# Three transformer blocks and a spectral block on one core: operands in one arena, V's bias folded away, LN in three parts, and every dense step for one image by a table of times

## The chip, the cores and the metric

The kernel runs on one core of a Trainium2 chip, in one launch. The time is the device time of an execution in microseconds; the figure shown is the median of several executions. The profile is of one further execution, taken by the hardware profiler. Its engines are TensorE (PE, with its weight loads as PEld), VectorE (DVE), ScalarE (ACT), GpSimd (POOL) and SyncE (SP), which here issues all DMAs.

## The reference

The input is x, 4 images of 16 x 16 tokens with 192 channels, in float32. Four blocks follow one another, each with its own weights.

```
for layer in (0, 1, 2):                 # head size 16, 48, 16; window 14, 16, 14
    y = layernorm(x) * g1 + b1
    q, k, v = split(windows(y) @ w_qkv + b_qkv)     # 12 heads
    a = (q * scale) @ k.T + rel_h(q)[..., None] + rel_w(q)[..., None, :]
    x = x + (softmax(a) @ v) @ w_proj + b_proj
    x = x + gelu((layernorm(x) * g2 + b2) @ w1 + b1) @ w2 + b2   # 192 -> 768 -> 192
# layer 3, spectral: rfft2 over the image, two complex 8-block matrices with biases,
# relu between them, soft shrink (0.01) after, inverse rfft2, added to x
```

With window 14 an image of 16 x 16 falls into one full window (196 tokens) and three that are mostly padding. Padded tokens are keys too: their k and v are the biases alone.

## The kernel before

Work goes in six phases: layers 0, 1 and 2, each for the first two images and then for the other two (`Phase`). Phases 0, 1, 4 and 5 have heads of 16 and windows of 14 (`L14`, `pads`), phases 2 and 3 have heads of 48 and one window of 16 (`L16`). Tokens of two images make 512 columns, four tiles of 128.

The steps of a phase are: `ln` (statistics, 1/sqrt by an integer guess and three Newton steps, normalisation, all on VectorE), `turn` (TensorE transposes, ScalarE writes XT with scale and bias), `q` and `k` (chunks of 96 columns of weights), `qs` and `ks` (each of q and k split in a high and a low part), `rel` (small matmuls with the relative positions), `aug` (SP copies the split parts and the relative terms of one head into its operand slot, QA and KA, beside rows of constants), `max` (scores once, VectorE takes the maxima of the rows), `maxT` (the maxima are transposed, and SP copies them as one more row, NR to QA), `scores` (scores again, less their maximum, and exp on ScalarE into PT), `pv`, `copy_o`, `inverse` and `divide` (output of a group of heads and its division by the sums), `norm` (the same for the last group), `proj`, the second `ln` and `turn`, `up`, `gelu`, `down`. The spectral block has `fwd`, `s1`, `s2`, `inv`, `out`.

Each engine takes its instructions in order, and all walk the same list of steps: `ordered()` (L298). A phase's frame is its scores, head by head; `attention_slots` hangs max (three heads ahead, or two), maxT, pv and aug on it; `beside(p)` spreads the tail of the phase before and the head of the next over the first three quarters, by costs written at each step. Where the layer changes (phases 2 and 4), `constants` and `prelude` come behind all of it: every row of constants, every slot's operands and the first maxima of the new layer are issued after the old layer's last scores. SP waits for those scores by name (L639 to L641, L682).

Slots: 6 for heads of 16, 4 for heads of 48, in two pairs of tensors (QA14 and KA14, QA16 and KA16) that share one place. Three banks of PSUM (`DENSE`) go round among the dense steps; two hold maxima, two scores, one the outputs.

The lines that matter below: L600 to L602 and L686 to L701 (weights, on the same SP queue as operands and rows), L766 (GpSimd permutes XT to XP for V and K of the 14-windows), L837 (K), L872 (exp), L890 and L896 (up, gelu), L899 (an Exp of two elements, which brings Exp's table back), L953 to L974 (LN), L980 (VectorE waits for the columns of layers 1 and 2), L1001 (V with its bias), L1005 to L1017 (q's split), L1043 (maxima), L1122 (every matmul).

Of the kernel before, what the change touches and what calls it, by code (L numbers as in the profile page):

```python
# [16 lines left out]
HB = 2  # L17
# [27 lines left out]
class Layer:  # L45


    def __init__(self, index, head_dim, window, eps, gelu):
# [150 lines left out]
def head_steps(p):  # L199

    L = PHASES[p].L
    out = [(("ln", 0, 0), 5.0), (("turn", 0, 0), 3.0)]
    if L.pads:
        out += [(("q", 0, 0), 1.0), (("k", 0, 0), 1.0), (("qs", 0, 0), 0), (("ks", 0, 0), 0), (("q", 1, 0), 1.5)]
        out += [(("rel", i, 0), 1.5) for i in range(3)]
    else:
        out += [(step, d) for step, d in unit_steps(0)]
    return out


def unit_steps(i):

    a, b = 2 * i, 2 * i + 1
    return [(("q", a, 0), 1.5), (("qs", a, 0), 0), (("q", b, 0), 1.5), (("k", a, 0), 1.5), (("ks", a, 0), 0),
            (("rel", i, 0), 2.0), (("qs", b, 0), 0), (("k", b, 0), 1.5), (("ks", b, 0), 0)]


def tail_steps(p):

    out = [(("proj", 0, 0), 1.5), (("proj", 1, 0), 1.5), (("ln", 1, 0), 5.0), (("turn", 1, 0), 3.0)]  # L220
    out += [(("up", m, 0), 1.5) for m in range(FM)]
    out += [(("gelu", 0, 0), 0), (("gelu", 1, 0), 4.0)]
    return out + [(("down", k, 0), 2.0) for k in range(2)]


def spectral_steps(s):
    out = [(("fwd", u, 0), 1.2) for u in range(4)] + [(("s1", u, 0), 1.2) for u in range(4)]
    return out + [(("s2", u, 0), 1.5) for u in range(4)] + [(("inv", t, 0), 1.5) for t in range(4)] + [(("out", 0, 0), 0)]


def beside(p):

    out = []
    if p:
        out += [((p - 1, *step), d) for step, d in tail_steps(p - 1)]
    if p % 2 == 0:
        out.append(((p, "weights", 0, 0), 0))
    if p == 5:
        out += [((4, *step), d) for step, d in spectral_steps(0)]
    if p + 1 < 6:  # L240
        out += [((p + 1, *step), d) for step, d in head_steps(p + 1)]
    return out


def attention_slots(p):

    L = PHASES[p].L
    slots = {(h, k): [(p, "scores", h, k)] for h in range(HEADS) for k in range(L.units)}
    joined = p + 1 < 6 and PHASES[p + 1].L is L
    for h in range(HEADS):  # L250
        g, first = h // L.per_group, h % L.per_group == 0
        if first and g:
            for k in range(L.units):
                slots[h, k].append((p, "pv", g - 1, k))
            slots[h, L.units - 1].append((p, "copy_o", g - 1, 0))
            slots[h + 1, 0].append((p, "inverse", g - 1, 0))
            slots[h + 1, L.units - 1].append((p, "divide", g - 1, 0))
        m = h + L.ahead
        where = (p, m) if m < HEADS else (p + 1, m - HEADS) if joined else None
        if where:  # L260
            for k in range(L.units):
                slots[h, k].append((where[0], "max", where[1], k))
            late = (h + 1, 0) if h + 1 < HEADS else (h, L.units - 1)
            slots[late].append((where[0], "maxT", where[1], 0))
        a = h + L.ring
        if a < HEADS:
            slots[h, L.units - 1].append((p, "aug", a, 0))
        elif joined and a - HEADS < L.ring:
            slots[h, L.units - 1].append((p + 1, "aug", a - HEADS, 0))
    if not L.pads:  # L270
        for i in range(1, 3):
            work = [(p, *step) for step, _ in unit_steps(i)]
            at = range(0, 4) if i == 1 else range(4, 12)
            for j, step in enumerate(work):
                k = at[j * len(at) // len(work)]
                slots[k // 2, k % 2].append(step)
    return [slots[h, k] for h in range(HEADS) for k in range(L.units)]


def prelude(p):  # L280

    L = PHASES[p].L
    out = [(p, "aug", h, 0) for h in range(L.ring)]
    for h in range(L.ahead):
        out += [(p, "max", h, k) for k in range(L.units)]
        if h:
            out.append((p, "maxT", h - 1, 0))
    return out + [(p, "maxT", L.ahead - 1, 0)]


FILL = [0.75] * 6


def second_chunk(p):
    return [(p, "k", 1, 0), (p, "qs", 1, 0), (p, "ks", 1, 0)] if PHASES[p].L.pads else []


def ordered():  # L298

    out = [(0, *step) for step, _ in head_steps(0)]  # L300
    out += prelude(0)
    for p in range(6):
        L = PHASES[p].L
        if p and PHASES[p - 1].L is not L:
            out += [(p, "constants", 0, 0), *prelude(p)]
        out += second_chunk(p)
        out += [(p, "v", t, 0) for t in range(L.vtiles)]
        slots, extra = attention_slots(p), beside(p)
# [33 lines left out]
def _build(nc, ctx, io, out):  # L342
# [180 lines left out]
    def split_rooms(L, c):  # L523

        if L.pads:
            return QHL14[:, :, :], KHL14[:, :, :]
# [892 lines left out]
```

## Time and profile before

| | |
|---|---|
| median of 3 runs | 798.07 us (797.04 to 798.78) |
| the profiled execution's own time | 794.48 us |
| its span, first to last instruction | 792.7 us |
| granted TensorE clock, mean over the span | 0.825 of full speed |
| HBM read and written | 10.09 MB and 0.79 MB |
| DMA bytes in all, mostly copies within the core | 51.73 MB |

The profile gives each engine's busy time and its share of the span. A wait is the idle time of an engine ahead of an instruction, put down to what came last. The granted clock is a share of TensorE's full 2.4 GHz; its other level is half of it. Every float32 matmul shows as two instructions, each with its weight load.

### The profile page before, as it was taken

Reading aid. Unit: us, or ns where it says so; the run is one execution under the profiler, and the core shown is the slowest. Engines: PE = TensorE matmul, PEld = TensorE weight load, DVE = VectorE, ACT = ScalarE, POOL = GpSimd, SP = SyncE. Lnnn points to the kernel's source line nnn. Section 1 sums busy time; section 2 is a strip of 40 time slices with the busy share of each in tenths; the row PEclk is TensorE's granted clock in tenths of the full one; section 3 lists DMA queues with packets and bytes.
Section 4 is the critical chain, followed back from the end, with each engine's and each line's share of the span. In section 5 each row is a group of like instructions: output and inputs, shape, how many; then the busy total and the mean of one; then the engine's idle time right before and its main releaser. Section 6 shows DMA issues by size and latency. Waiting matters only on the chain.

```text
span 792.7 us, 13858 instructions
## 1 busy us (share of the span) xinstructions
PE 601.9 (76%) x5444; PEld 434.8 (55%) x5444; DVE 314.9 (40%) x846; ACT 224.7 (28%) x420; POOL 125.1 (16%) x154
## 2 busy tenths in 40 slices
PE   7737487797906988878989887387949667997677
PEld 4525365666605645645755655265726454785366
DVE  4325546526212521515242363535344652352203
ACT  2113231263400235213124433003523226222231
POOL 2120202000400231132032230010011210010001
PEclk8666756698856999979989997678986779997799
DMA  5582122130033122344022130612251302100000
GB/s 159 135 197 58 39 59 57 24 72 21 14 86 114 31 80 74 104 121 132 15 75 72 47 104 2 170 27 49 47 145 41 77 19 58 39 2 20 1 0 21
DMA packets 31913, 51.73 MB, mean 65 GB/s; under 512 B 8383, under 2 KB 12719, under 8 KB 31754
## 3 DMA queue, kind: packets, MB, share of 16 engines
q1 hardware_dynamic: 31850, 50.85, 24.8%
q8 instruction: 44, 0.72, 0.4%
q14 instruction: 19, 0.16, 0.1%
HBM read 10.09 MB, written 0.79 MB: 14 GB/s over the span
## 4 chain that ended last, share of the span: by engine, by line
PE 59%; DVE 16%; SPq 8%; DMA 7%; issue 5%; ACT 5%; DVEq 0%; POOL 0%; ACTq 0%
PE PS L1122 56%; DVE NM L1043 3%; DMA QA<-NR 3%; DMA COL<-in_col 2%; DVE STAT L954 2%; PE PS L1140 1%; DMA QA<-KC 1%; SPq L615 1%; PE PS L1214 1%; DVE XN L973 1%; DVE QHL L1016 1%; ACT HT L896 1%; SPq L654 1%; SPq L648 1%; DVE RSTD L965 1%
## 5 line engine op out<-in xcount | busy, mean ns | idle before, releaser
L872 ACT ACTIVATE PT<-PS 98x392 f32<-98x392 f32 (+2 forms) x192 | 96.2, 513 | 319.1 <-PE PS L1122 318.6
L1043 DVE TENSOR_REDUCE NM<-PS 98x2 fp32r<-98x392 f32 (+2 forms) x192 | 108.1, 572 | 146.4 <-PE PS L1122 145.0
L1122 PE MATMUL PS<-QA,KA 128*98 128x196 f32 (+2 forms) x528 | 124.8, 348 | 28.3 <-DMA QA<-NR 20.3
L1122 PE MATMUL PS<-KA,QA 127*98 127x196 f32 (+3 forms) x432 | 105.5, 344 | 48.5 <-issue 33.9
L1122 PEld LDWEIGHTS PS<-QA,KA 128*98 128x98 f32 (+2 forms) x528 | 89.9, 212 | 58.5 <-issue 24.7
L1122 PEld LDWEIGHTS PS<-KA,QA 127*98 127x98 f32 (+3 forms) x432 | 72.8, 217 | 69.8 <-issue 50.2
L1122 PE MATMUL PS<-XT,W 96*128 96x512 f32 x144 | 69.9, 620 | 1.3 <-ACT XT L817 1.3
L1122 PE MATMUL PS<-XT,WQKV 96*96 96x512 f32 x128 | 64.7, 635 | 1.3 <-ACT XT L817 1.3
L1214 PE MATMUL PS<-IDN,NM 120*6 120x120 f32 (+1 forms) x72 | 22.9, 318 | 54.4 <-DVE NM L1043 54.4
L1122 PE MATMUL PS<-PT,V 128*32 128x196 f32 (+2 forms) x672 | 60.6, 407 | 0.9 <-ACT PT L872 0.9
L1122 PE MATMUL PS<-W,HT 128*128 128x192 f32 x288 | 52.6, 343 | 10.9 <-ACT HT L896 10.9
L1122 PEld LDWEIGHTS PS<-W,HT 128*128 128x128 f32 x288 | 50.2, 202 | 13.6 <-ACT HT L896 12.6
L771 POOL TENSOR_TENSOR OT<-OS,OT 128x512 f32<-128x512 f32 x18 | 23.0, 1276 | 205.7 <-DVE OT L1061 205.6
L1051 DVE CAST NR<-PS 5x120 fp32r<-5x120 f32 (+1 forms) x72 | 19.0, 264 | 63.0 <-PE PS L1214 56.1
L1122 PEld LDWEIGHTS PS<-XT,W 96*128 96x128 f32 x144 | 27.1, 199 | 28.5 <-issue 26.6
L1122 PE MATMUL PS<-Q,RB 32*32 32x32 f32 (+1 forms) x2304 | 37.7, 225 | 5.0 <-issue 4.1
L1214 PEld LDWEIGHTS PS<-IDN,NM 120*6 120x6 f32 (+1 forms) x72 | 5.9, 83 | 61.5 <-DVE NM L1043 61.5
L1122 PEld LDWEIGHTS PS<-Q,RB 32*32 32x32 f32 (+1 forms) x2304 | 34.8, 126 | 8.6 <-issue 7.5
L1122 PEld LDWEIGHTS PS<-PT,V 128*32 128x32 f32 (+2 forms) x672 | 28.4, 137 | 18.5 <-issue 6.7
L1122 PE MATMUL PS<-WP,OT 128*128 128x192 f32 x192 | 36.0, 351 | 3.0 <-DVE OT L1075 3.0
L1122 PEld LDWEIGHTS PS<-WP,OT 128*128 128x128 f32 x192 | 35.1, 210 | 4.2 <-issue 4.2
L890 ACT ACTIVATE HT<-PS,COL 128x512 f32<-128x512 f32 x36 | 24.7, 687 | 43.0 <-PE PS L1122 43.0
(91 smaller groups left out, 663.2 us busy)
## 6 DMA issues: line engine op xcount, KB each, us to landing
QA<-QHL SPq DMA_DIRECT2D x72, 96.0 KB, 2.4
KA<-KHL SPq DMA_DIRECT2D x48, 141.0 KB, 2.6
QA<-REL SPq DMA_DIRECT2D x48, 128.0 KB, 2.4
QA<-QHL SPq DMA_DIRECT2D x24, 192.0 KB, 2.7
KA<-KHL SPq DMA_DIRECT2D x24, 192.0 KB, 2.7
W<-in_w SPq DMA_DIRECT2D x6, 576.0 KB, 6.5
QA<-REL SPq DMA_DIRECT2D x48, 64.0 KB, 2.2
KA<-KC SPq DMA_DIRECT2D x12, 235.0 KB
```

The costliest lines, as they stand in the source:

```text
L615: sp.dma_start(raw(KA16[row:end, tile, s, :]).rearrange("r (b t) -> r b t", b=HB), KC16[L.rel_row:L.rel_row + size, :].unsqueeze(1).broadc ...
L648: sp.dma_start(raw(QA14[0:3 * hd, 0, s, :]), raw(qhl[mine, :, :])).then_inc(aug_in[s].sem, 16)
L654: sp.dma_start(raw(KA14[0:3 * hd, 0, s, :]), raw(khl[mine, :, :])).then_inc(aug_in[s].sem, 16)
L771: nc.gpsimd.tensor_tensor(OT[:, i, :], OS[:, :], OT[:, i, :], ALU.mult).then_inc(o_done.sem, 1)
L872: nc.scalar.activation(dst, src, ACT.Exp).then_inc(probs_done.sem, 1)
L890: nc.scalar.activation(HT[:, i, :], PS[:, bank[0], :], ACT.Identity, bias=COL[n][:, b1:b1 + 1])\
L896: nc.scalar.activation(part, part, L.gelu).then_inc(gelu_done.sem, 1)
L954: ins = nc.vector.bn_stats(STAT[:, t, :], X[:, t0 + t, :])
L1043: nc.vector.tensor_reduce(dst, src, AX.X, ALU.max, negate=True).then_inc(max_done.sem, 1)
L1051: nc.vector.tensor_copy(NR[0:cols, h % 2, 0:L.max_rows], PS[0:cols, bank[0], 0:L.max_rows])\
L1122: return nc.tensor.matmul(dst, lhsT, rhs, start=start, stop=stop, skip_group_check=loose)
L1214: nc.tensor.transpose(PS[0:cols, bank[0], 0:rows], NM[n][0:rows, h % 2, 0:cols].bitcast(F32), IDN[0:rows, 0:rows]).then_inc(maxT_psum.sem, 1)
```

## The change

The diff replaces the order of the steps, the place of the operands and the split of several steps.

1. **Order.** `head_steps`, `tail_steps`, `beside`, `attention_slots`, `prelude` and `second_chunk` go. A table `TIMES` holds for each phase and step the times at which its instances stand, in heads, counted from 12p; `scores` stand at h + k / units. `ordered()` sorts by them.
2. **One image.** `ln`, `turn`, `up`, the first two chunks of `q` and the first of `k` are done for one image (256 columns) at a time, as is `s1`. The gelus of the two images are separate, each with its return to Exp. ScalarE evacuates up of the first image, VectorE that of the second. XT1 is one tensor in place of two. The spectral block has its own room (LATE) for each half.
3. **Arena.** Operand slots of both layers lie in one tensor, 5 for heads of 48 and 6 for heads of 16, so that a new layer's slot waits only for the old heads that lie under it. Constants are laid slot by slot (a pair of slots in one DMA for heads of 16). Q and K parts of a head of 16 go in one DMA.
4. **Fold.** V's bias is no longer added to V. It is multiplied into the projection (`fold`) and added to the row of its bias; the padded values become zeros and a one.
5. **Split normalisation.** `ln` is VectorE's statistics, `rs` GpSimd's 1/sqrt, `xn` ScalarE's normalisation. `norm` is two steps.
6. K of the 14-windows is made from unpermuted columns and permuted as ScalarE writes it; V of these layers is written by ScalarE. PT16 has four rooms in place of two. X's second half and the columns of layers 1 and 2 are loaded at phase 0's `weights` step, ahead of the weights. The memsets of PT14 go.

```diff
-        self.ring = 6 if self.pads else 4
+        self.ring = 6 if self.pads else 5
+        self.turn = 2 if self.pads else 3
+        self.slot_room = self.tiles * (HT_ + self.keys)
-        self.aug_dmas = 3 if self.pads else 6
+        self.aug_dmas = 2 if self.pads else 6
...
+def place_of(p, h):
+    L = PHASES[p].L
+    return (HEADS * (p % 2) + h + L.turn) % L.ring
+
+def slot_start(L, s):
+    return L16_ROOM - (L.ring - s) * L.slot_room
...
+TIMES = [
+    {"ln": (-7.429, -7.238, 13.611, 14.190,),
+     "rs": (-7.810, -7.048, 13.889, 14.286,),
+     "xn": (-7.619, -6.667, 14.143, 14.513,),
...
+     "k": (-6.476, -4.762, 0.444,),
...
+     "v": (-0.571, 0.167, 1.042, 1.083, 1.208,),
+     "weights": (2.889,),
...
+    {"ln": (-8.917, -6.200, 13.700, 14.417,),
...
+     "aug": (-4.167, -3.067, -2.111, -1.111, -0.111, 0.200, 1.190, 2.095, 3.111, 4.143, 5.133, 6.250,),
...
+     "constants": (-2.800, -1.933, -1.600, -0.111, 0.125,),
+     "aug": (-2.733, -1.733, -1.222, 0.312, 0.929, 1.900, 2.812, 3.750, 4.938, 5.577, 6.889, 7.700,),
...
+def ordered():
     out = []
+    for p, table in enumerate(TIMES):
         L = PHASES[p].L
+        scores = tuple(h + k / L.units for h in range(HEADS) for k in range(L.units))
+        for step, times in [("scores", scores), *table.items()]:
+            out += [(HEADS * p + t, (p, step, *part)) for t, part in zip(times, parts(L, step, len(times)))]
+    return [step for _, step in sorted(out, key=lambda timed: timed[0])]
...
             elif step == "constants":
-                sp.wait_ge(*scores_psum.at(p - 1, HEADS * PHASES[p - 1].L.units - 1))
-                lay_constants(ph)
+                s = place_of(p, h)
...
+                over = last_over(p, s) if p else None
...
+                if over is not None:
+                    sp.wait_ge(*scores_psum.at(p - 1, PHASES[p - 1].L.units * (over + 1) - 1))
+                if not L.pads or h % 2 == 0:
+                    lay_constants(L, s)
...
+            elif step == "rs":
+                pool.wait_ge(*mean_var[i].at(p, u))
+                two_tiles = slice(2 * u, 2 * u + 2)
+                var, rstd, sq = VAR[:, two_tiles], RSTD[:, two_tiles], SQ[:, two_tiles]
+                link(nc.gpsimd.tensor_scalar(var, MV[:, two_tiles, 1], L.eps, None, ALU.add))
+                link(nc.gpsimd.tensor_scalar(rstd.bitcast(I32), var.bitcast(I32), -0.5, float(0x5F3759DF),
+                                             ALU.mult, ALU.add))
+                for _ in range(3):
+                    link(nc.gpsimd.tensor_tensor(sq, rstd, rstd, ALU.mult))
+                    link(nc.gpsimd.tensor_tensor(sq, sq, var, ALU.mult))
+                    link(nc.gpsimd.tensor_scalar(sq, sq, -0.5, 1.5, ALU.mult, ALU.add))
+                    link(nc.gpsimd.tensor_tensor(rstd, rstd, sq, ALU.mult))
+                link(nc.gpsimd.tensor_tensor(sq, rstd, MV[:, two_tiles, 0], ALU.mult))
+                nc.gpsimd.tensor_scalar(sq, sq, -1.0, None, ALU.mult).then_inc(rstd_done[i].sem, 1)
...
+            if step == "xn":
+                act.wait_ge(*rstd_done[s].at(p, u))
...
+                for t in range(2 * u, 2 * u + 2):
+                    nc.scalar.activation(XN[:, t, :], X[:, ph.tile0 + t, :], ACT.Identity, scale=RSTD[:, t:t + 1],
+                                         bias=SQ[:, t:t + 1]).then_inc(xn_done[s].sem, 1)
...
             elif step == "gelu":
-                if i == 0:
-                    act.wait_ge(*up_done.at(p, FM - 1))
+                act.wait_ge(*up_done[i].at(p, FM - 1))
...
-                if i == 1:
-                    nc.scalar.activation(LOADED[:, :], COL[0][:, 0:2], ACT.Exp)
+                nc.scalar.activation(LOADED[:, 1 + 2 * p + i, :], COL[0][:, 0:2], ACT.Exp)
...
+            elif step == "up" and u == 1:
+                dve.wait_ge(*up_psum.at(p, FM + i))
+                nc.vector.tensor_scalar(HT[:, i, TOK:], PS[:, bank[0], 0:TOK], COL[n][:, b1:b1 + 1], None, ALU.add)\
+                    .then_inc(up_done[1].sem, 1)
+            elif step == "fold":
+                dve.wait_ge(*fold_psum.at(p, 0))
+                nc.vector.tensor_tensor(WP[rows, 0, :], WP[rows, 0, :], PS[rows, bank[0], 0:C], ALU.add)\
+                    .then_inc(fold_done.sem, 1)
```

## Rows read from the trace of the kernel before

**Rows 1.** The page's first part: busy us, share of the span, instructions
```profile
PE 601.9 (76%) x5444; PEld 434.8 (55%) x5444; DVE 314.9 (40%) x846; ACT 224.7 (28%) x420; POOL 125.1 (16%) x154
```
**Rows 2.** Windows by stage (one without matmuls left out): us, busy us per engine, clock, DMA share, GB/s
```profile
0.00:64.50 64.50, 35.19 (x488) 23.54 (x488) 26.97 (x96) 10.16 (x23) 12.24 (x34) 0.69 0.60 151
64.50:218.60 154.10, 123.87 (x1300) 92.97 (x1300) 71.45 (x180) 56.31 (x117) 23.41 (x25) 0.75 0.20 45
...
242.60:498.70 256.10, 222.63 (x2028) 153.56 (x2028) 98.48 (x263) 76.34 (x126) 58.93 (x61) 0.91 0.25 73
498.70:525.20 26.50, 11.63 (x34) 6.54 (x35) 15.09 (x26) 0.98 (x2) 3.66 (x3) 0.63 0.55 137
525.20:726.60 201.40, 158.52 (x1394) 121.78 (x1394) 86.28 (x232) 66.79 (x133) 22.27 (x26) 0.85 0.20 49
726.60:792.70 66.10, 50.08 (x200) 36.41 (x200) 14.17 (x45) 14.09 (x19) 4.54 (x5) 0.87 0.02 6
```
**Rows 3.** Waits of TensorE: engine line, for whom, us in total, times, longest
```profile
PE PS L1214 <- DVE NM L1043: 54.4, 29, 18.3
PE PS L1122 <- issue: 46.0, 10, 24.0
PE PS L1122 <- DMA QA<-NR: 20.3, 8, 7.7
PE PS L1122 <- DVE V L1001: 13.4, 4, 6.1
PE PS L1122 <- ACT HT L896: 10.9, 5, 3.6
```
**Rows 4.** Timeline, start: start us, us, engine, line, what, idle before, releaser
```profile
37.22 3.64 PE L1122 MATMUL PS<-XP,WQKV 96*96 96x512 f32 x4
...
40.65 3.85 PE L1122 MATMUL PS<-WQKV,XP 96*98 96x192 f32 x20
...
44.78 0.88 ACT L872 ACTIVATE PT<-PS 98x392 f32<-98x392 f32 x2 [2.83 <-PE PS L1122]
```
**Rows 5.** The chain of waits, then the timeline, behind phase 0's weights
```profile
45.21 13.10 DMA COL<-in_col
...
64.53 0.36 PE L1214 MATMUL PS<-IDN,NM 120*6 120x120 f32 x1 [18.30 <-DVE NM L1043]
```
**Rows 6.** Timeline at the boundary to phase 2: an issue of SP, TensorE's wait
```profile
236.67 0.61 SPq L650 DMA_DIRECT2D QA<-QHL  x1
...
242.60 2.05 PE L1122 MATMUL PS<-KA,QA 128*128 128x256 f32 x8 [24.04 <-issue]
```
**Rows 7.** Timeline, second chunk's split in phase 1
```profile
95.12 0.36 PE L1214 MATMUL PS<-IDN,NM 120*6 120x120 f32 x1 [9.80 <-DVE NM L1043]
```
**Rows 8.** Timeline, first and last of the six waits for an LN
```profile
153.18 0.36 PE L1214 MATMUL PS<-IDN,NM 120*6 120x120 f32 x1 [5.32 <-DVE NM L1043]
...
738.58 2.08 PE L1140 MATMUL PS<-IDN,XN 128*96 128x128 f32 x8 [5.12 <-DVE XN L973]
```
**Rows 9.** Timeline of ScalarE at a gelu
```profile
172.38 1.28 ACT L896 ACT_TABLE_LOAD   x1
...
173.68 2.86 ACT L896 ACTIVATE HT<-HT 128x1536 f32<-128x1536 f32 x2
```
**Rows 10.** Timeline: a load of up, and 128 Q,RB matmuls twice
```profile
751.31 0.19 PEld L1122 LDWEIGHTS PS<-XT,W 96*128 96x128 f32 x1 [0.24 <-issue]
...
101.38 2.12 PE L1122 MATMUL PS<-Q,RB 32*32 32x32 f32 x128
...
271.47 2.06 PE L1122 MATMUL PS<-Q,RB 96*32 96x32 f32 x128
```
**Rows 11.** Groups by form: count, busy us, mean ns, idle before
```profile
L973 DVE TENSOR_SCALAR XN<-X,MV,RSTD 128x192 f32<-128x192 f32 x48 | 15.0, 376 | 0.4
```
**Rows 12.** GpSimd: a memset in the timeline, and a group by form
```profile
59.28 0.12 POOL L734 MEMSET BV<- 120x12 f32 x1
...
L786 POOL TENSOR_SCALAR W1N<-WS 96x192 f32<-96x192 f32 x1 | 0.7, 692 | 15.3 <-DMA SB<-in_sb 15.3
```

More of the change, by code:

```diff
@@ L218, in tail_steps @@
[L218 to L228, printed above, removed]
@@ L231, in beside @@
-def beside(p):
-    out = []
[L234 to L277, printed above, removed]
@@ L280, in prelude @@
[L280 to L302, printed above, removed]
-        L = PHASES[p].L
[L304 to L308, printed above, removed]
-        whole, at, placed = sum(d for _, d in extra) / FILL[p], 0.0, []
-        for step, d in extra:
-            placed.append((at / whole * len(slots), step))
-            at += d
-        for j, slot in enumerate(slots):
-            out += slot
-            while placed and placed[0][0] < j + 1:
-                out.append(placed.pop(0)[1])
-        out += [step for _, step in placed]
-        out += [(p, "pv", L.groups - 1, k) for k in range(L.pv_steps)] + [(p, "norm", 0, 0)]
-    out += [(5, *step) for step, _ in tail_steps(5)]
-    return out + [(5, *step) for step, _ in spectral_steps(1)]
@@ L323, with last_over @@
-BANKS = {"turn": 2, "q": 1, "k": 1, "rel": 1, "maxT": 1, "proj": 1, "up": 1, "down": 1, "fwd": 1, "s1": 1, "s2": 1,
+    return (HEADS * (p % 2) + h + L.turn) % L.ring
+def slot_start(L, s):
+    return L16_ROOM - (L.ring - s) * L.slot_room
+L16_ROOM = LAYERS[1].ring * LAYERS[1].slot_room
+def last_over(p, s):
+    L, before = PHASES[p].L, PHASES[p - 1].L
+    first, end = slot_start(L, s), slot_start(L, s) + L.slot_room
+    over = [h for h in range(HEADS - before.ring, HEADS)
+            if slot_start(before, place_of(p - 1, h)) < end
+            and slot_start(before, place_of(p - 1, h)) + before.slot_room > first]
+    return over[-1] if over else None
@@ new lines, in parts @@
+def parts(L, step, n):
+    if step in ("max", "scores", "pv"):
+        per_head = L.pv_steps if step == "pv" else L.units
+        return [divmod(j, per_head) for j in range(n)]
+    if step in ("ln", "rs", "xn", "turn"):
+        return [divmod(j, HB) for j in range(n)]
+    if step == "up":
+        return [(m, b) for b in range(HB) for m in range(FM)]
+    if step == "q":
+        return [(c, b) for b in range(HB) for c in range(2)] + [(c, HB) for c in range(2, L.chunks)]
+    if step == "k":
+        return [(0, b) for b in range(HB)] + [(c, HB) for c in range(1, L.chunks)]
+    return [(j, 0) for j in range(n)]
@@ L351, in _build @@
     XN = sb(ctx, "XN", [128, 4, C])
-    XT1 = [sb(ctx, f"XT1_{half}", [CK, 2, HT_]) for half in range(2)]
+    XT1 = sb(ctx, "XT1", [CK, 2, HT_])
     XT2 = sb(ctx, "XT2", [CK, 2, HT_])
@@ L541, in values @@
     def values(L, t, h):
-        rows = EDGES if L.pads and t == 2 * HB else 128
+        rows = 128 if not L.pads else HALF_IN if t < 2 * HB else EDGES
         return V[L.index][0:rows, t, h * L.vcol:h * L.vcol + L.slot]
@@ L966, in _ @@
[L966 to L984 removed]
+                ins.then_inc(mean_var[s].sem, 1)
@@ L1384, in _pack @@
         place[0, L.sum_row, 0] = bp
+        vb = np.zeros((L.per_group, L.slot, L.groups, L.sum_row + 1), np.float32)
+        bv = bqkv[2 * L.dim:].reshape(L.groups, L.per_group, L.hd).transpose(1, 2, 0)
+        for row, first, end in L.spans:
+            vb[:, row:row + end - first, :, L.sum_row] = bv[:, first:end]
         rb = np.zeros((pairs, L.hd, 2, 2, L.rel_room, 2), np.float32)
```

688 lines of the change are left out of this document (437 added, 251 removed).

## The prediction

> **What bounds the kernel now.** I read the page's first part, then the stages by windows, then TensorE's waits, then the timeline at each long wait. Over the 792.7 us span TensorE is busy 601.9 us, no other engine as much as 315 [rows 1]. So 190.8 us are TensorE's idle time. The windows cut the span where the work changes: start, phases 0 and 1, phases 2 and 3 (head size 48), the boundary to phase 4, phases 4 and 5, and the tail [rows 2]; between the second and the third lie 24.0 us without a matmul [rows 6]. The reader is to see two things in them: how much of each TensorE stands, and that the granted clock goes with how closely TensorE is fed: 0.69 and 0.75 in the first two stages, 0.91 in phases 2 and 3, where it is busy 87% of the time. Busy time times granted clock, summed over the six rows, is 24.3 + 92.9 + 202.6 + 7.3 + 134.7 + 43.6 = 505 us: what the same matmuls would take at 2.4 GHz. So 97 us of the busy time are the lower clock's. The two prizes are thus 191 us idle and 97 us of slow clock; beneath them lie some 505 us of work that the change hardly touches.
>
> The waits say who leaves TensorE idle [rows 3]: mostly VectorE's maxima (54.4 us in 29 waits), because VectorE takes its instructions in order and something else stands ahead of them; then "issue" (46.0 in 10), which is above all the two boundaries; then the row of maxima that comes by DMA (20.3), VectorE's copies of V (13.4) and the gelu (10.9).
>
> **The change part by part**, against the profiled execution (794.48 us, of which 792.7 span). Table entries are in heads: phase p counts from 12p, and one head takes about 6 us in phases 0, 1, 4, 5 and 10 us in 2 and 3 (201.4 and 154.1 us for about 24 heads each, 256.1 for 24).
>
> *Start.* The first exp is at 44.8; ahead of it stand the maxima of three heads, K's second chunk (3.64 us of matmul) and the V tiles (3.85 us) [rows 4]. By phase 0's table, K chunk 1 (0.444) and four of five V tiles (0.167 and later) come behind the first scores (0.0): -6.7 us. Six constant DMAs in place of twelve and a K that no longer waits for the permuted copy give some 2 more. I take **-9**; bounds 0 (the maxima alone set it) and -14 (twice what the two parts give).
>
> *Weights of phase 0.* TensorE idles 18.3 us up to 64.5, since VectorE waits 13.1 us for the column biases, queued behind weights [rows 5], and then does phase 1's LN before the maxima. Now X's second half and the columns are issued first (2.889), and VectorE's statistics wait (3.083) for X alone. But the weights still go by the one SP queue, and the next rows of maxima (maxT of head 5 at 3.167) queue behind them: the same megabytes held the queue for 13 us. I take **-10**, bounds -4 (13 of them return as waits for the row) and -16.
>
> *Boundaries.* 24.0 us at 218.6 [rows 6], and 14.9 idle in the 26.5 us behind 498.7 [rows 2]: all constants of the new layer, then all operands, wait for the old layer's last scores. In the arena, slots are freed one by one: phase 2's first head lies over L14 slots 2 to 4, free after head 8, the second over 4 and 5, free after head 9, the third over none; constants start at -2.8 and operands at -2.73. What remains is SP: three constant and six operand DMAs for each L16 head, at 0.61 us of issue and 0.03 between them [rows 6], are 5.8 us a head beside about 3 that an L14 head needs, in 6 us. So SP falls some 3 us behind with each of three heads: 9 us late on the 24, which leaves -15. At the second, whose new heads need less of SP, I take 10 of the 14.9: **-25**; bounds -10 (SP also waits in order for scores) and -36 (nearly all of both).
>
> *Second chunk's split, V, and XP.* 9.8 us at 85.3 [rows 7] are VectorE waiting for head 5's operand DMA before it may overwrite the split rooms, and then the split; the V copies cost 13.4 [rows 3], and about 6 us of "issue" are a wait for the permuted copy. V's copies go to ScalarE, K needs no permuted input. The room still waits for head 5 (issued at 0.2, split at 0.56 to 0.61, that is 2 us later with a landing of 2.5), so half stays: 29 us in all, **-14**; bounds -6 and -24.
>
> *LN.* A whole LN holds VectorE for about 5.3 us; six waits, of which the first and the last are shown, come to 30.4 [rows 8], and I add 4.5 for phases 2 and 3, where they are shorter. Now VectorE does only the statistics, for one image at a time (4 of the 24 instructions that held it, so about 0.9 us), GpSimd the 16 small operations, ScalarE the four normalisations. **-24** of 34.9; bounds -10 and -38.
>
> *Gelu.* Each image gets its own gelu and its own way back to Exp, so there are 12 more table loads at 1.28 us [rows 9], 15.4 us of ScalarE, which is idle 72% of the time. Waits for the gelu cost 10.9 us of TensorE now [rows 3]. The first gelu comes earlier, the second load costs again: **+6**, bounds 0 and +15 (nothing hidden). Here a page speaks against the change. The row shows the load from 172.38 and the gelu from 173.68, 1.30 us. The Trainium skill (ScalarE: Activation LUTs, What ACT_TABLE_LOAD costs) adds about 1.38 us of drain to each switch, 2.66 us in all. By that the twelve would be 32 us and my +6 about +12; the trace has no such gap, so the row is taken.
>
> *More and smaller matmuls.* Up goes from 12 to 24 matmuls a phase, q and the first k likewise, s1 from 16 to 32: with the fold some 270 instructions over 5444. At 2.4 GHz a 512-column pass has a pitch of 0.43 us (load 0.19, then 0.24 idle) [rows 10], so 256 columns take 0.215 and still cover the load. Taken as **0**; it would be +8 (0.03 each) were loads in the open. The six folds are in the last term.
>
> *Tail.* From 726.6 to the end 66.1 us, 50.1 busy. Phase 4's spectral part (16 fwd, 16 s1, 32 s2 and 32 inv instructions a half, at about a weight load's 0.2 us [rows 10] some 20 us of TensorE) moves from beside phase 5's heads (11.4 to 21.7 in phase 5's table) into the tail, whose holes come to 66.1 - 50.1 = 16 us [rows 2], 5.1 of them the LN [rows 8]. 20 us leave phase 5 and about 10 come back beyond the holes: **-10**, bounds 0 and -20.
>
> *What ScalarE takes over.* 48 normalisations (15.0 us on VectorE at 376 ns), 20 V copies, split turns, K in three pieces, less up's second image [rows 11]: some 25 us by an estimate from that 376 ns beside the table loads, on an engine that works in order between exps. The normalisation waits for GpSimd's chain. The nearest GpSimd rows are 0.12 us (memset 120x12) and 0.69 (96x192, one operand) [rows 12]; nearest in size is the first, so 16 x 0.15 to 0.2 = 2.4 to 3.2 us, against 0.35 to 0.45 head, 2 to 2.7 us, that the tables leave between the two steps. About 0.3 us late, 24 times, with the folds and the copies: **+11**, bounds 0 and +35. Beside it: the Trainium skill (GPSIMD Engine Reference, Performance versus the Vector engine) advises against GpSimd for elementwise work, at 1.96 times VectorE's time on large tiles; no row of before shows it at two columns.
>
> *Clock.* If every stage is fed as phases 2 and 3 are now, it gets their 0.91: 505 / 0.91 = 555 in place of 602, -47; less some 7, because the Q,RB matmuls take 2.1 us for 128 at either clock [rows 10]: **-40**. Bounds -10 (the waits move rather than go) and -65.
>
> Sum: -9 -10 -25 -14 -24 +6 +0 -10 +11 -40 = -115, or 679.5 us for a profiled execution. The median of the runs shown, 798.07, is 3.6 above the profiled 794.48, so I predict **683 us**.
>
> **The rivals.** *A: the waits go and the clock stays.* The same sum without the clock term gives 719.5, 723 as a median. For it: phases 4 and 5 have 21% idle and 0.85, so the clock isn't bound to a single long wait. Against: the clock is highest where the idle share is lowest. *B: TensorE becomes the whole limit.* 505 us of work, 15 for Q,RB and the like, and idle time of 35 at the start, 15 at boundaries, 20 in the tail and 5 in each of six phases give 620, 624 as a median. For it: no other engine passes 40%. Against: the chains exp, PV, maxima and SP's order stay. *C: ScalarE waits in order for GpSimd, and the kernel gets slower.* Place: step "xn", 24 times, each ahead of an exp that TensorE needs. If a GpSimd operation costs 0.69 us even at two columns, the chain is 11.0 us against 2.5 allowed: 8.5 late, of which some 2 are covered by the two score banks. 24 x 6.5 = 156, less the 7 already counted: 683 + 149 = 832. It passes "before" from a chain of about 9.3 us, 0.58 us an operation. For it: ScalarE and TensorE have at most two banks between them. Against: the memsets at 0.12. *D: the written order itself misfits* (SP at the boundaries, rows of maxima behind weights): half of the idle time returns elsewhere; 115 / 2 gives 741.
>
> **How the numbers follow.** 0.45 for my forecast (its own range 655 to 705), 0.20 for B, 0.17 for A, 0.11 for D, 0.07 for C. The range 632 to 742 leaves out most of C and the outer ends of B and D. Faster: everything but C, 0.93, less 0.01 for a chance landing within 0.2% (1.6 us, about what can be told from no change): faster 0.92, same 0.01, slower 0.07.
>
> **What would show it.** Right: no TensorE wait over 12 us at the two boundaries; VectorE's maxima end under 25 us of waits in place of 54; the first exp before 38 us; some 5700 matmul instructions; granted clock about 0.9 over the span; TensorE's busy time near 560. Wrong: a clock below 0.86 (A); xn instructions whose idle time before them is GpSimd's and longer than 2 us each (C); waits for the row of maxima above 35 us in all, or SP issuing without a break across the boundaries while TensorE stands (D). The sum fails if the tail grows by more than phase 5 loses.

## The result, and the profile after

The changed kernel takes 760.3 us (median of 4 runs, 758.13 to 764.34) against 797.59 of the kernel before beside it, a ratio of 0.9536 [0.9495, 0.9578]. The forecast was 683 with a range of 632 to 742: the direction was right, the size was a third. The profiled execution took 760.11 us. Now and then an execution is over 1.5% slower than the fastest of its kernel, mostly at a lower granted clock: times and ratios below (a ratio with its 95% interval) are of the others, and only the profiles of the wide relative terms (clock 0.822) and of the loads from ScalarE's queue (0.612) are of such executions.

The page's first part, columns as in [rows 1]:

```profile
span 758.3 us, 14860 instructions
PE 615.0 (81%) x5716; PEld 484.3 (64%) x5716; DVE 273.3 (36%) x671; ACT 279.5 (37%) x580; POOL 199.8 (26%) x540
```

TensorE's idle time fell from 190.8 us to 143.3, by 47.5. Its busy time rose by 13.1, though the forecast had it fall by 40. The granted clock is 0.835 over the span, against 0.825. The windows of the kernel after, columns as in [rows 2], cut at the first exp, inside phases 0 and 1, at the first boundary, at the first and last exp of phases 2 and 3, at the first and last exp of phases 4 and 5:

```profile
0.00:42.90 42.90, 30.04 (x467) 23.73 (x467) 10.77 (x36) 11.69 (x31) 13.74 (x54) 0.66 0.44 101
42.90:147.50 104.60, 70.64 (x801) 53.68 (x801) 44.70 (x108) 33.77 (x89) 21.94 (x54) 0.66 0.39 88
147.50:227.30 79.80, 68.08 (x545) 54.30 (x544) 26.19 (x70) 36.18 (x73) 23.35 (x75) 0.85 0.16 37
227.30:256.50 29.20, 23.75 (x255) 15.09 (x254) 8.77 (x20) 4.90 (x10) 5.03 (x5) 0.82 0.38 109
256.50:491.60 235.10, 205.10 (x1917) 157.70 (x1917) 84.95 (x199) 92.05 (x166) 80.33 (x187) 0.91 0.31 86
491.60:494.60 3.00, 1.40 (x10) 0.84 (x10) 1.53 (x4) 0.34 (x3) 0.00 (x0) 1.00 0.63 139
494.60:682.00 187.40, 153.16 (x1349) 122.95 (x1351) 74.48 (x185) 79.25 (x171) 42.09 (x123) 0.83 0.25 57
682.00:758.30 76.30, 62.86 (x388) 55.98 (x378) 21.89 (x51) 21.31 (x40) 13.34 (x42) 0.95 0.04 11
```

The kernel before had the same events at 44.8 (first exp), 260.1, 496.6, 528.5, 721.6 and 792.7. So the start is 1.9 us shorter, phases 0 and 1 with the first boundary 1.7 (213.6 against 215.3), phases 2 and 3 1.4, the second boundary 28.9 (3.0 against 31.9), phases 4 and 5 5.7, and the tail 5.2 longer. In sum 34.4, most of it at the second boundary, where the idle time fell from 15.1 us to 1.6 and some 15 us of TensorE's work now stand in other stages.

TensorE's waits after, columns as in [rows 3]:

```profile
PE PS L1320 <- ACT XN L983: 30.3, 12, 6.4
PE PS L1303 <- DMA ARENA<-NR: 26.8, 10, 12.8
PE PS L1395 <- DVE NM L1212: 21.5, 12, 6.2
PE PS L1303 <- issue: 21.0, 19, 5.3
PE PS L1303 <- DVE NM L1212: 11.3, 13, 2.6
```

The maxima's 54.4 us are 21.5, under the 25 of the forecast, and "issue" is 21.0 in place of 46.0, no wait of it over 5.35. The first exp (42.9, to be under 38), the clock and the busy time missed their signs. The first line is new: the transposes of the "turn" step wait for the normalisation. On ScalarE that is a wait for GpSimd, in the kernel after's groups (count, busy us, mean ns, idle before):

```profile
L983 ACT ACTIVATE XN<-X,SQ,RSTD 128x192 f32<-128x192 f32 x48 | 23.6, 538 | 68.2 <-POOL SQ L936 68.1
```

One of the 24 chains, in the timeline of the kernel after (start, length, engine; "..." stands for 13 more of GpSimd's operations of 0.19 or 0.20 us; work of other engines in between, and lines between the last three, are left out):

```profile
521.97 0.25 DVE L1147 BATCH_NORM_AGGREGATE MV<-STAT 128x2 f32<-128x6 f32 x2
522.31 0.22 POOL L927 TENSOR_SCALAR VAR<-MV 128x2 f32<-128x2 f32 x1 [17.81 <-DVE MV L1147]
522.61 0.19 POOL L928 TENSOR_SCALAR RSTD<-VAR 128x2 int32<-128x2 int32 x1
...
526.49 0.22 POOL L936 TENSOR_SCALAR SQ<-SQ 128x2 f32<-128x2 f32 x1
526.75 0.98 ACT L983 ACTIVATE XN<-X,SQ,RSTD 128x192 f32<-128x192 f32 x2 [4.72 <-POOL SQ L936]
527.87 1.06 PE L1320 MATMUL PS<-IDN,XN 128*96 128x128 f32 x4 [6.43 <-ACT XN L983]
530.40 6.33 PE L1303 MATMUL PS<-XT,W 96*128 96x256 f32 x16
537.38 1.97 PE L1303 MATMUL PS<-XT,W 96*128 96x256 f32 x8
```

Sixteen operations of two columns follow one another every 0.276 us (0.20 at work, 0.08 between), from 522.31 to 526.71: 4.4 us, and the other 23 chains take as long. ScalarE and TensorE take their steps in order, and both stand meanwhile. Of the 24 chains ScalarE waited for 17, TensorE for 12. The reader is to look at the last two lines too. The first 16 matmuls of up behind the wait take 0.396 us each, the next 8 of the same form 0.246. The windows around that place say why (same columns as above):

```profile
517.00:521.40 4.40, 4.40 (x30) 4.19 (x28) 1.05 (x3) 0.26 (x1) 0.00 (x0) 1.00 0.00 0
521.40:527.90 6.50, 0.07 (x2) 0.06 (x2) 2.10 (x11) 1.61 (x4) 3.20 (x17) 0.83 0.25 58
527.90:532.00 4.10, 4.10 (x16) 3.76 (x17) 1.52 (x3) 1.37 (x3) 3.14 (x12) 0.50 0.00 0
532.00:536.00 4.00, 4.00 (x11) 3.13 (x11) 0.00 (x0) 1.95 (x5) 2.00 (x6) 0.51 0.00 0
536.00:540.00 4.00, 4.00 (x25) 3.47 (x24) 0.45 (x2) 3.08 (x8) 0.00 (x0) 1.00 0.01 1
```

Full clock, a wait of 6.4 us, then 1.2 GHz for 8 us in which TensorE never stops, then 2.4 again. So the wait is paid for twice, and dense work stands behind it: up here, q/k elsewhere. They are the groups that carry the extra busy time, up at 79.1 us after (69.9 before) and q/k at 100.1 (86.6 before).

### The profile page after: what moved, and what is told of

Its sections match the earlier page's. It is cut to its first block, busy times and chain, and to the rows that moved or that the text cites. A ratio compares the mean times of both kernels' runs of the same rounds, so it can differ in the third digit from the quotient of the medians.

```text
span 758.3 us, 14860 instructions
## 1 busy us (share of the span) xinstructions
PE 615.0 (81%) x5716; PEld 484.3 (64%) x5716; DVE 273.3 (36%) x671; ACT 279.5 (37%) x580; POOL 199.8 (26%) x540
## 4 chain that ended last, share of the span: by engine, by line
PE 60%; DMA 9%; issue 8%; SPq 8%; DVE 6%; POOL 5%; ACT 3%; DVEq 0%; ACTq 0%; POOLq 0%
PE PS L1303 56%; DMA ARENA<-NR 4%; DMA ARENA<-REL 4%; PE PS L1320 2%; ACT XN L983 1%; DVE QKHL L1185 1%; PE PS L1395 1%; DVE NM L1212 1%; SPq L790 1%; DMA ARENA<-KC 1%; SPq L810 1%; DVE QKHL L1180 1%; POOL SQ L932 1%; SPq L812 1%; POOL RSTD L934 1%
## 5 line engine op out<-in xcount | busy, mean ns | idle before, releaser
L1303 PE MATMUL PS<-ARENA 128*128 128x256 f32 (+4 forms) x960 | 193.3, 339 | 52.3 <-DMA ARENA<-NR 26.8
L1303 PEld LDWEIGHTS PS<-ARENA 128*128 128x128 f32 (+4 forms) x960 | 149.0, 215 | 88.5 <-issue 33.2
L1303 PE MATMUL PS<-XT,WQKV 96*96 96x256 f32 (+1 forms) x232 | 100.1, 577 | 9.1 <-issue 7.8
L1303 PE MATMUL PS<-XT,W 96*128 96x256 f32 x288 | 79.1, 423 | 5.5 <-ACT XT L993 4.6
L1303 PEld LDWEIGHTS PS<-XT,W 96*128 96x128 f32 x288 | 59.1, 214 | 18.8 <-ACT XT L993 6.1
L1303 PEld LDWEIGHTS PS<-XT,WQKV 96*96 96x96 f32 x232 | 45.7, 212 | 38.4 <-issue 28.4
L1303 PE MATMUL PS<-PT,V 98*32 98x196 f32 (+2 forms) x672 | 57.1, 381 | 1.8 <-ACT PT L1051 1.8
L983 ACT ACTIVATE XN<-X,SQ,RSTD 128x192 f32<-128x192 f32 x48 | 23.6, 538 | 68.2 <-POOL SQ L936 68.1
L1320 PE MATMUL PS<-IDN,XN 128*96 128x128 f32 x96 | 20.6, 355 | 31.1 <-ACT XN L983 30.3
L1303 PE MATMUL PS<-Q,RB 32*32 32x32 f32 (+1 forms) x2304 | 38.5, 225 | 7.7 <-issue 6.4
L1395 PE MATMUL PS<-IDN,NM 120*6 120x120 f32 (+1 forms) x72 | 22.2, 310 | 22.9 <-DVE NM L1212 21.5
L1303 PEld LDWEIGHTS PS<-PT,V 98*32 98x32 f32 (+2 forms) x672 | 26.0, 127 | 19.7 <-issue 8.7
```

Source lines behind the costliest of these rows:

```text
L983: nc.scalar.activation(XN[:, t, :], X[:, ph.tile0 + t, :], ACT.Identity, scale=RSTD[:, t:t + 1], bias=SQ[:, t:t + 1]).then_inc(xn_done[s]. ...
L1303: return nc.tensor.matmul(dst, lhsT, rhs, start=start, stop=stop, skip_group_check=loose)
L1320: last = nc.tensor.transpose(PS[0:CK, bank[0], k * TOK + t * 128:k * TOK + (t + 1) * 128], XN[:, 2 * u + t, k * CK:(k + 1) * CK], IDN[:, :])
L1395: nc.tensor.transpose(PS[0:cols, bank[0], 0:rows], NM[n][0:rows, h % 2, 0:cols].bitcast(F32), IDN[0:rows, 0:rows]).then_inc(maxT_psum.sem, 1)
```

## The experiments

The theory after the comparison: GpSimd's chain makes the normalisation late, 24 times, and the lower clock behind each wait doubles the loss. The rival: such waits only move, and the clock is held down by something else (the small matmuls, the halved dense steps). All kernels are edits of the kernel after unless said otherwise; a ratio is to the kernel before beside it.

**Chain of 4 operations.** The three Newton steps are left out, so 1/sqrt is only the first guess.

```diff
-                for _ in range(3):
+                for _ in range(0):
                     link(nc.gpsimd.tensor_tensor(sq, rstd, rstd, ALU.mult))
```

> The kernel after, with the three Newton steps of 1/sqrt left out (so the normalisation keeps only the first guess): GpSimd's chain is 4 operations in place of 16, about 1.1 us in place of 4.4, 24 times. Theory 1 (the chain is what makes ScalarE's normalisation late, and TensorE stands and then runs at the lower clock): TensorE's waits for XN fall from 30.3 us to under 8, ScalarE's for GpSimd from 68 to under 15, the granted clock rises to 0.86 or more, the time falls by 35 us or more, to 725 or less. Theory 2 (TensorE's waits only move to the next late thing, and the clock has another cause): the XN waits go likewise, but others grow, the clock stays at 0.83 to 0.845 and the time stays at 745 or more.

720.4 us, 0.9054 [0.9022, 0.9086]: 40 us less for twelve operations a chain (38 by the ratios, each to the kernel before beside it).

```profile
span 717.3 us, 14572 instructions
PE 597.7 (83%) x5716; PEld 471.4 (66%) x5716; DVE 270.6 (38%) x671; ACT 278.7 (39%) x580; POOL 143.7 (20%) x252
```

The waits for XN are 8.0 us in place of 30.3, TensorE's idle time 119.6 in place of 143.3, and its busy time 597.7 in place of 615.0: 23.7 us of waits and 17.3 of busy time. The waits did not move elsewhere: the idle time fell by as much as XN's waits did (22.3) and a little more. Of the 17.3, 15.4 are the clock: TensorE is busy at 1.2 GHz for 169.3 us in place of 200.1, by the clock's records in the traces. ScalarE's waits for GpSimd are 23.7 us in place of 68.1 and the clock is 0.852: neither reaches what theory 1 asked (under 15, and 0.86). The place shown above, now in this run's timeline:

```profile
495.99 1.03 PE L1320 MATMUL PS<-IDN,XN 128*96 128x128 f32 x4 [3.12 <-ACT XN L983]
496.67 2.02 PE L1303 MATMUL PS<-ARENA 127*98 127x196 f32 x8
498.49 4.09 PE L1303 MATMUL PS<-XT,W 96*128 96x256 f32 x16
```

The wait is halved, and the same 16 matmuls of up take 4.09 us, not 6.33. The first exp comes at 35.8, not 42.9: the start too was waiting for chains.

**Chain of 12** (two Newton steps).

> The kernel after with two Newton steps in place of three: a chain of 12 operations, some 3.3 us in place of 4.4, a dose between the kernel after (16) and the run with 4, which was 40 us faster. If the time goes with the chain's length: a third of it, 13 us, so 745 to 750. If only chains beyond some length hurt: the gain is all at the first operations taken away, 735 or less, or none of it, 757 or more.

736.2 us, 0.9274 [0.9215, 0.9333]: 24 us for the first 4 operations (21 by the ratios), so more than half of the 40. XN's waits are 22.6 us. Neither answer fits exactly: it pays at both steps, and more for each operation at the longest chain.

**Chain on VectorE**, behind its own statistics (12 linked operations).

> The kernel after, with one part undone: the 1/sqrt chain stands on VectorE behind its own statistics again, per image (12 linked operations in place of GpSimd's 16), the normalisation stays on ScalarE. Theory 1: XN waits of 30.3 us fall to under 12, while VectorE is held some 2 us longer 24 times, of which a part shows as waits for the maxima; net gain of 10 to 25 us, 735 to 750. Theory 2 (VectorE's in-order hold costs as much as GpSimd's latency did): 755 to 775, with the waits for VectorE's maxima above 50 us.

754.4 us, 0.9474 [0.9435, 0.9513], between the two answers. On VectorE the same chain is shorter, an operation each 0.197 us (12 operations from 516.98 to 519.31):

```profile
516.98 0.17 DVE L1139 TENSOR_SCALAR VAR<-MV 128x2 f32<-128x2 f32 x1
...
519.15 0.16 DVE L1146 SCALAR_TENSOR_TENSOR SQ<-RSTD,MV 128x2 f32<-128x2 f32 x1
```

XN's waits fell to 12.4 us, but the two lines of waits for VectorE's maxima rose from 21.5 and 11.3 to 24.3 and 31.0. So a latency is traded for a hold.

**One chain on each**: image 0's on VectorE, image 1's on GpSimd beside it.

> The kernel after with the first image's 1/sqrt chain on VectorE behind its statistics (11 linked operations, 2.2 us by the run with all chains on VectorE) and the second image's on GpSimd, beside it. Theory 1: the first image's chain is the one TensorE waits for, and the second's is covered by the first's dense steps; XN waits 30 to 8 to 14 us, VectorE is held half as often as with all chains on it: 740 to 750. Rival: the waits for VectorE's maxima grow by what XN's fall: 754 or more.

750.7 us, 0.9426 [0.9392, 0.9459]; XN 12.4, maxima 24.5 and 24.0.

**Filled waits.**

```diff
                 claim(bank[0], xt_done[s].at(p, 2 * u + 1))
+                for _ in range(6):
+                    mm(PS[:, bank[0], 0:128], WARM[:, :], WARM[:, :], True, True)
```

> The kernel after, with six matmuls of constant 128x128 data (by the 28 at the start, 6.14 us, about 1.3 us for six) ahead of each of the 24 turns, between the claim of the bank and the wait for XN: 31 us of useless work, of which some 14 lie in the 12 waits for XN. Theory 1 with a clock that follows the gaps: the filled waits leave no half clock behind, which gives back about as much as the fill costs, 755 to 768. Rival (the clock doesn't depend on these gaps): the whole uncovered fill shows, 772 to 785, at a clock that stays 0.83 to 0.84.

762.5 us, 0.9552 [0.9473, 0.9631]: not to be told from the kernel after. Some 36 us more of useless matmuls (288 instructions, at the 0.127 us of those in the timeline below) cost nothing, the clock is 0.866, and q/k are 85.9 us in place of 100.1, up 74.6 in place of 79.1. XN's waits are 14.7. At the place shown above:

```profile
521.21 1.52 PE L1303 MATMUL PS<-WARM 128*128 128x128 f32 x12
527.71 1.09 PE L1322 MATMUL PS<-IDN,XN 128*96 128x128 f32 x4 [4.98 <-ACT XN L983]
528.45 2.02 PE L1303 MATMUL PS<-ARENA 127*98 127x196 f32 x8
530.26 3.44 PE L1303 MATMUL PS<-XT,W 96*128 96x256 f32 x12
```

The 36 us are an estimate at full clock; the group of these matmuls is busy 48.8 us in place of 6.1, and yet TensorE's busy time in all rose only from 615.0 to 626.9, of which 158.4 in place of 200.1 at 1.2 GHz. This is the direct evidence that the clock is lost in these gaps: more work, no more time.

**Wide relative terms.** In the window layers, 64 matmuls of 32 columns become 8 of 256.

> The kernel after; in the window layers each rel step's 64 small matmuls (32 rows, 32 columns) are replaced by 8 of 256 columns over the same input, so the relative terms are other values. If the small matmuls pull the clock down behind them (the trace has 0.50 after several of these stretches): less time than the matmuls alone save, the clock rises above 0.85 and the time falls by 20 us or more, to 740 or less. If the clock follows the idle gaps only: the time falls by what these matmuls take less (12 steps, at most 1 us each), 745 to 760, and the clock stays.

747.4 us, 0.9383 [0.9329, 0.9438]: 13 us less. That is what the matmuls themselves may be worth (the groups' busy time is 24.4 us in place of 38.5), so the small matmuls aren't what holds the clock: this part of the rival falls. (The run's relative terms are other values.)

**Gelus joined.** Both at the second one's place, one return to Exp.

> The kernel after, with one part undone: both images' gelu stand together, at the second one's place, and the table goes to Gelu and back once per phase instead of twice: 12 loads of 1.28 us (15 us of ScalarE) gone, the down projection waits a little longer. If the second table change is what it cost: 5 to 8 us faster, 752 to 756. If ScalarE's loads are hidden beside TensorE: 758 to 762. If the early first gelu was worth more than its load: slower, 763 to 768.

767.0 us, 0.9605 [0.9530, 0.9680]: 7 us slower by the medians, with intervals that overlap, so not shown. TensorE waits 10.3 us for the gelu again, as in [rows 3], where the kernel after has no such line. The 15.4 us of loads on ScalarE, gone here, brought no gain, so they were hidden.

**Up for both images at once**, on top of the joined gelus.

```diff
-                    last = mm(PS[:, bank[0], 0:TOK], W1[:, k, i * 128:(i + 1) * 128], XT2[:, k, tokens_of(u)],
+                    last = mm(PS[:, bank[0], :], W1[:, k, i * 128:(i + 1) * 128], XT2[:, k, :],
```

> The kernel before this one in the list (gelus joined), with up's matmuls for both images at once again: 144 of 512 columns in place of 288 of 256, evacuated by VectorE alone, after both images are turned. The trace has up at 79.1 us busy in 288 instructions, against 69.9 in the kernel with 144. If halving the columns costs TensorE real time: 8 to 12 us less than the joined gelus alone. If the difference of 9 us is only the granted clock in those stretches, or the later start of up eats it: within 4 us of the joined gelus, or slower.

788.2 us (two executions), 0.9897 [0.9795, 0.9999]: 21 us slower than the joined gelus. The two groups, the joined kernel's first:

```profile
L1305 PE MATMUL PS<-XT,W 96*128 96x256 f32 x288 | 75.1, 405 | 5.2 <-ACT XT L994 3.0 <-ACT HT L1081 1.2 <-ACT LATE L1100 0.9
```

```profile
L1306 PE MATMUL PS<-XT,W 96*128 96x512 f32 x144 | 74.9, 662 | 2.4 <-ACT XT L995 2.4
```

Halving the columns costs TensorE nothing. What it buys is cover: with up of both images behind both turns, the waits for XN are 50.4 us in 17 in place of 30.1 in 12, and these 20.3 us are all that TensorE's idle time grew by (147.5 to 167.8). Up by image is worth some 21 us because one image's up stands under the other's chain; the edit also gives all of up's copies to VectorE, which was not separated.

**Loads of phase 0's weights step from ScalarE's queue.**

> The kernel after, with all loads of phase 0's weights step but X's second half issued from ScalarE's queue in place of SP's, so that the rows of maxima no longer stand behind them in one queue. If the wait of 12.8 us for a row of maxima at 72.6 is the order of one queue: it falls under 4 us, and the time by 8 to 16 us, to 745 to 752. If it is the bytes (the rows' packets share the same DMA engines with 3.6 MB whatever the queue): the wait stays above 8 us and the time within 4 us of 760. ScalarE's 15 issues at 0.45 to 1.9 us are some 10 us on its queue and cost up to 6 back.

756.7 us, 0.9536 [0.9468, 0.9605]. The longest wait for a row of maxima is 3.1 us, not 12.8, which points to the order in one queue (with TensorE at 0.612 each row is needed later, so the two waits are not strictly alike); but a wait of 9.8 for ScalarE's exp stands in its place, and the ratio is that of the kernel after. The Trainium skill (DMA: Bandwidth & Descriptors, Queues, rings and completion order) says that each DMA engine goes round between the queues that have work, a packet at a time; these two waits agree.

**Layer 1's QKV weights in six pieces behind heads 8 to 13.**

> The kernel after, with only what phase 0 needs soon (projection, up and down weights, columns) loaded at its weights step; the 1.3 MB of layer 1's QKV weights go in six pieces behind the operands of heads 8 to 13, its constants and the biases behind heads 14 and 15. If bytes ahead of the row of maxima are the cause: the wait of 12.8 us falls to some 6 (about half of the bytes are gone) and the pieces cost at most 1 us each where they pass: 750 to 756. If the count of issues on SP is the cause (each about 0.5 us, 5 us gone): the wait falls by the same 5 or so but the six pieces, one at a time, cost nothing. If the later waits absorb it: 758 to 762.

752.8 us (two executions), 0.9462 [0.9400, 0.9524], the row's wait 8.0. Beside the kernel after's 0.9536 that is anything from no gain to 11 us.

**Columns first, in the kernel before.**

```diff
+        for k in (1, 2):
+            sp.dma_start(COL[k][:, :], io[f"col{k}"]).then_inc(col_in[k].sem, 16)
```

> The kernel before with one part of the change: the column biases of layers 1 and 2 are loaded behind X's second half, at the start, and not behind phase 0's weights. TensorE's 18.3 us wait at 46 us began with VectorE's 13.1 us wait for them. If that was its cause: the wait falls to some 5 us and the time by 10 to 16. If the row of maxima behind the same weights takes its place, as in the kernel after: 8 us or more of it come back as a wait for the row, and the time falls by under 6.

784.1 us, 0.9842 [0.9802, 0.9881]: 11.5 us less than before from this one edit. The wait of [rows 5] is now:

```profile
54.54 0.36 PE L1215 MATMUL PS<-IDN,NM 120*6 120x120 f32 x1 [5.50 <-DVE NM L1044]
```

**Put together.** Hybrid chains of two Newton steps with the spread QKV weights:

> The last kernel with two Newton steps (chains of 8 operations on VectorE, 12 on GpSimd) and with layer 1's QKV weights in six pieces behind heads 8 to 13. If the gains add: another 12 to 20 us, 722 to 735. If they overlap (the same clock or the same waits): 738 to 745.

730.8 us, 0.9183 [0.9141, 0.9224]. Then all weights in pieces, with two steps on GpSimd alone, on both engines, and on GpSimd with the fill:

> The kernel after with two Newton steps on GpSimd, and with all weights of phase 0 and layer 1's QKV weights in pieces of 288 KB or less, one behind each head's operands from head 7 to head 17; only X's second half, the columns and small tables stay at the weights step. If the weights' bytes ahead of the rows of maxima hold phases 0 and 1: against 736.2 with two steps alone, the 11.9 us wait is gone and 8 to 15 us with it, 721 to 728. If the pieces only move the waits to other rows: 732 to 738.

> The same loads with the first image's chain on VectorE and the second's on GpSimd, two steps both. If the place of the chain matters as much as its length: 5 to 12 us under the kernel before it in the list. If VectorE's hold costs what GpSimd's latency does: within 4 us of it. Against 730.8 with a part of the loads spread: 2 to 8 us less, as the longest wait for a row there was already down to 5.7 us.

> The first kernel of this list with the six useless matmuls (1.3 us) ahead of each turn. With a chain of 16 they cost nothing net (762 against 760) and raised the clock from 0.835 to 0.866. With a chain of 12 the waits for XN are 22.6 us in place of 30.3, so fewer of the fills are covered: 3 to 10 us slower than unfilled, at a clock 0.01 to 0.02 higher. If it is faster than unfilled, the clock behind the remaining waits is worth more than 31 us of work.

728.7 us, 0.9137 [0.9091, 0.9182]; 727.9 us, 0.9124 [0.9055, 0.9193]; and 737.1 us, 0.9217 [0.9149, 0.9284]. So the simple edit does as well as the hybrid, and with a shorter chain the fill no longer pays, though the clock is 0.874 (the intervals touch). The three of 728 to 731 us can't be told apart; all beat both kernels. In the hybrid with all loads spread the longest wait for a row is 5.8 us, yet its window from 36 to 120 us still has a clock of 0.66 and 61.6 us busy in 84.

## Why the prediction was wrong

Two steps failed: the clock term, and the lateness of GpSimd's chain. Without the clock term the sum had TensorE's idle time fall by 75 us and its busy time by nothing; with it the busy time was to fall by 40. Measured, the idle time fell by 47.5 and the busy time rose by 13.1, so 27.5 us of the miss are idle time and 53.1 busy time.

**The chain (0.3 us late, 24 times, in the ScalarE term of +11, against LN's -24).** VectorE's waits for an LN went, but 30.3 us came back as waits for XN, of the 34.9 to be won. The chain was taken as 16 x 0.15 to 0.2 = 2.4 to 3.2 us, from a memset [rows 12]; it is 4.4, as the 0.08 us between two linked operations was left out. ScalarE stood 68.1 us for it, 2.8 a chain and not 0.3: the 2 to 2.7 us that the tables leave between the two steps weren't there. At the place shown ScalarE waits 4.72 us. The short chain prices the whole: 38 to 40 us, 24 of idle time and 17 of busy time. The better row was at hand: VectorE's own chain, inside the LN of [rows 8], ran from 149.10 to 151.49 in the kernel before, 12 linked operations at 0.2 us, so 16 on the slower engine could not be under 3.2. The normalisation takes 538 ns, where VectorE took 376 [rows 11]. The Trainium skill (ScalarE: Activation LUTs, What ACT_TABLE_LOAD costs) gives an ACTIVATE 186 ns + 0.833 ns per column and 93 ns for each pointer operand, an estimate of 532 ns for 192 columns and two pointers; the trace agrees. Rival C had the place, the engine and the test ("xn instructions whose idle time before them is GpSimd's and longer than 2 us": 68.1 us in 17, 4.0 each), but only as the case of 0.69 us an operation. By its own sum 0.276 would cost nothing (4.4 less the 2.5 allowed and the 2 covered); measured, it cost a quarter of C's 156 us, because neither the allowance nor the cover was there. (C's threshold of 9.3 us leaves out the 7 already counted; by its own terms it is 9.6.)

**Clock (-40) is the larger failure, and the chain is the smaller part of it.** The span's clock is 0.835, under the 0.86 that was to speak for rival A. By the clock's records TensorE was busy at 1.2 GHz for 183.4 us before and for 200.1 after. The new waits stand ahead of dense steps, and clock is lost there: 17 of the 53 us, as the short chain shows. The other 36 stay with the short chain too. There the idle time fell by 71.2 us, nearly the 75 of the sum, and the busy time by 4.2 only; 720.4 us is rival A's 723, not 683. So of the 77 us between 683 and 760 the chain holds 40 and the clock term's own error 37. The term took every stage to be fed as phases 2 and 3. The stages between the exps, with the short chain, from phase 0 to phase 3 and then 4 and 5 (columns as in [rows 2]):

```profile
35.80:126.60 90.80, 59.59 (x723) 44.71 (x722) 34.94 (x89) 29.30 (x78) 13.37 (x27) 0.65 0.42 94
126.60:243.70 117.10, 103.45 (x877) 76.54 (x876) 41.95 (x109) 45.48 (x93) 22.81 (x35) 0.84 0.23 58
243.70:463.90 220.20, 195.62 (x1913) 152.05 (x1914) 84.56 (x198) 91.11 (x165) 61.63 (x91) 0.94 0.33 92
466.90:571.70 104.80, 83.10 (x874) 68.02 (x873) 43.27 (x108) 43.18 (x97) 18.32 (x36) 0.80 0.32 75
571.70:644.50 72.80, 65.27 (x464) 51.99 (x467) 31.20 (x77) 35.55 (x74) 9.68 (x15) 0.88 0.18 39
```

Phase 0 still stands 34% of its time at 0.65 and phase 4 21% at 0.80; only phases 2 and 3 have 0.94. The forecast's own sum left 116 us idle in 683, 17%, where phases 2 and 3 had 13%, so 0.91 all over did not follow from it. Which waits of phases 0 and 4 hold the clock down there was not tested and stays open.

**Start (-9):** 1.9 measured; with the short chain the first exp is at 35.8, the forecast 9 earlier. The term was right for a chain that is not late; these 7 us are part of the 40.

**Weights of phase 0 (-10):** the 18.3 us wait [rows 5] became one of 12.8 for the row of maxima that SP issued at 74.32, behind the weights:

```profile
85.41 0.64 PE L1303 MATMUL PS<-ARENA 128*98 128x196 f32 x2 [12.82 <-DMA ARENA<-NR]
```

The waits differ by 5.5 us, inside the bounds, with the cause that they named. In the kernel before the columns alone gave 11.5.

**Boundaries (-25):** better than forecast, some 32. The 24.0 us of [rows 6] are 5.35, and TensorE's idle time at the second boundary is 1.6 in place of 15.1. SP did issue without a break, for 21.8 us from 222.08 and some 6.6 us for a head of phase 2, as was reckoned; but it started early enough that 5.35 us of it show, not 9. Still phases 0 and 1 with their boundary gained only 1.7 us: TensorE's idle time there fell by 23 (74.1 to 51.1), its busy time rose by 21 (141.2 to 162.5). By the clock's records 18 of these 21 are more work (at full clock 106.7 before, 124.3 after), such as that of phase 2 which now stands earlier, and 4 the clock.

**Second chunk, V, XP (-14):** the 13.4 us for V are gone, but the reading of [rows 7] was wrong. SP issued the operands of phase 0's last head, 11, from 84.96 to 86.28, and what then waited for them was the split of phase 1's first chunk; its wait is 1.63 now. The second chunks were split ahead of the first scores before, with no wait. Now they come behind them and wait for the room, as here in phase 0:

```profile
50.61 1.18 DVE L1180 CAST QKHL<-Q 96x392 fp32r<-96x392 f32 x3 [4.62 <-DMA ARENA<-REL]
...
55.54 0.36 PE L1395 MATMUL PS<-IDN,NM 120*6 120x120 f32 x1 [6.15 <-DVE NM L1212]
```

In phase 1 it is 5.10 us and in phase 4 4.88: 16 us of the 21.5 that are left of the maxima's waits. The term had half of 9.8 stay.

**Gelu (+6)** probably had the wrong sign: two gelus save what the joined kernel waits (10.3 us) and their loads are hidden, some 7 us to the good by medians, not clear of the noise. Each of the 24 loads takes 1.28 us in the groups, and no 2.66 us can be seen; the trace agrees with the row, as weighed.

**More and smaller matmuls (0)** was right: 75.1 against 74.9 us. **Tail (-10)** was wrong by the stages: phases 4 and 5 lose 5.7 us and the tail gains 5.2, so the moved spectral half seems to save nothing; no run has it alone.

## What to carry to other kernels

When a chain of small linked operations moves to another engine, count its pitch, not its busy time, and put the whole latency against the work that stands between its start and its use; a shorter chain (here one Newton step less, 21 to 24 us) was worth more than another engine (6 us). Don't book a better clock as the reward of fewer waits: here 71 us less idle time gave 4 us of it. A wait ahead of dense matmuls costs it again in clock, so look at what stands right behind a wait, and try other work under it. Splitting a dense step by image pays through such cover, not through TensorE's own time.

## What the hardware showed that was not expected

- The same chain is an operation each 0.276 us on GpSimd and 0.197 on VectorE, at two columns: 1.4 times, with 0.08 and 0.04 us of it between two operations.
- Behind a wait of 6.4 us TensorE ran at 1.2 GHz for 8 us of unbroken work; across the run with the short chain 23.7 us less idle came with 17.3 us less busy time.
- Some 36 us of added matmuls in such waits left the time where it was (762.5 against 760.3).
- From the first exp to 120 us the clock stayed at 0.66 in the run with all loads spread (longest wait for a row 5.8 us), as over 42.9 to 147.5 in the kernel after (12.8 us); why stays open.
